# Two graph-attention layers on one core: the softmax's shift and sum folded into 12 segment-wise exponentials, moved to the head of ScalarE's step

## The reference: what is computed

```python
q, k, v = split_heads(x @ Wq + bq), split_heads(x @ Wk + bk), split_heads(x @ Wv + bv)
scores = einsum('bhqd,bhkd->bhqk', q, k) / sqrt(32) + beta * adj
scores = where(adj > 0, scores, -9e15)
x = layernorm(x + einsum('bhqk,bhkd->bhqd', softmax(scores), v))          # layer 0

a = einsum('bnhd,bmhd->bhnm', x @ Wq.T, x @ Wk.T) * 384 ** -0.5 + adj
a = nan_to_num(softmax(where(all(a == 0, axis=-1), -inf, a)))
x = layernorm(x + einsum('bhnm,bmhd->bnhd', a, x @ Wv.T + bv) @ Wo.T + bo)  # layer 1
```

## Time and profile before

| | |
|---|---|
| device time, median of 3 runs | 1110.32 us (1110.06 to 1113.08) |
| device time of the profiled execution | 1110.85 us |
| its span, first to last instruction | 1109.1 us |
| TensorE matmuls busy | 1063.5 us (96%) |
| VectorE busy | 936.5 us (84%) |
| GpSimd busy | 528.7 us (48%) |
| ScalarE busy | 444.9 us (40%) |
| mean granted TensorE clock | 0.985 |

### The profile page before, as it was taken

How to read it: one execution, slowest core, us unless ns; L and a number is a source line. 1 busy time by engine, 2 the same in 40 slices (tenths; PEclk the granted TensorE clock), 3 DMA queues, 4 the chain that set the end, 5 groups by cost and what they waited for, 6 DMA issues and landing times.

```text
span 1109.1 us, 38264 instructions
## 1 busy us (share of the span) xinstructions
PE 1063.5 (96%) x16896; PEld 917.9 (83%) x16896; DVE 936.5 (84%) x1642; ACT 444.9 (40%) x713; POOL 528.7 (48%) x454
## 2 busy tenths in 40 slices
PE   4789999999999999999999999999999999999975
PEld 3678888888888888888888888888888888888864
DVE  2468998998989899898989989898898989978785
ACT  3334443444344343444433444444444434444321
POOL 0135454454545546454454645445364544655443
PEclk8989999999999999999999999999999999999997
DMA  8103111112112011111102111111211210010101
GB/s 265 39 2 97 50 59 43 38 45 64 37 43 59 26 54 46 42 53 49 49 26 64 38 43 59 43 38 45 64 38 43 59 36 15 17 35 2 40 24 37
DMA packets 61749, 53.32 MB, mean 48 GB/s; under 512 B 35984, under 2 KB 55440, under 8 KB 61584
## 3 DMA queue, kind: packets, MB, share of 16 engines
q1 hardware_dynamic: 60752, 49.69, 15.1%
q10 hardware_dynamic: 832, 1.18, 0.3%
HBM read 38.28 MB, written 12.58 MB: 46 GB/s over the span
## 4 chain that ended last, share of the span: by engine, by line
PE 90%; DVE 4%; issue 2%; DMA 2%; ACT 1%; POOL 1%; SPq 0%; POOLq 0%; DVEq 0%; ACTq 0%
PE ps_u L340 53%; PE ps_s L357 9%; PE ps_o L340 8%; PE ps_p L425 7%; PE ps_p L440 7%; PE ps_x L370 3%; PE ps_o L454 2%; DMA xt_in<-in_x_t 1%; DVE probs L620 1%; POOL probs L756 1%; DMA bo_rows<-in_bo 1%; DVE row_sum L668 1%; DVE xt_lo L648 1%; ACT probs L547 0%; DVE row_max L630 0%
## 5 line engine op out<-in xcount | busy, mean ns | idle before, releaser
L756 POOL TENSOR_TENSOR probs<-probs,row_max 128x768 f32<-128x768 f32 x128 | 209.8, 1639 | 323.0 <-DVE row_max L630 323.0
L762 POOL TENSOR_TENSOR probs<-probs,row_inv 128x768 f32<-128x768 f32 x128 | 188.6, 1474 | 128.8 <-DVE row_inv L676 69.5
L516 ACT COPY probs_t<-ps_p 128x768 f32<-128x768 f32 x128 | 102.6, 802 | 201.3 <-PE ps_p L425 201.2
L340 PE MATMUL ps_u<-w_hi_v,xt_lo 128*128 128x384 f32 x384 | 138.4, 360 | 7.0 <-DVE v_sb L661 5.4
L668 DVE TENSOR_REDUCE row_sum<-probs 128x12 f32<-128x768 f32 x128 | 121.6, 950 | 24.4 <-ACT probs L547 23.6
L547 ACT ACTIVATE probs<-probs 128x768 f32<-128x768 f32 x128 | 108.4, 847 | 83.0 <-POOL probs L756 83.0
L340 PE MATMUL ps_u<-xt_hi,w_lo_k 128*128 128x512 f32 x288 | 119.0, 413 | 11.6 <-ACT q_sb L535 6.3
L340 PE MATMUL ps_u<-w_hi_v,xt_hi 128*128 128x384 f32 x384 | 129.9, 338 | 0.0
L340 PE MATMUL ps_u<-w_lo_v,xt_hi 128*128 128x384 f32 x384 | 129.8, 338 | 0.0
L775 POOL TENSOR_TENSOR rstd<-var_eps,minus_half 128x1 f32<-128x1 f32 x128 | 69.9, 546 | 124.9 <-DVE var_eps L709 124.9
L630 DVE TENSOR_REDUCE row_max<-probs 128x12 f32<-128x768 f32 x128 | 121.4, 948 | 2.2
(11 more groups left out here) (78 smaller groups left out, 2033.4 us busy)
## 6 DMA issues: line engine op xcount, KB each, us to landing
x_in<-in_x SPq DMA_DIRECT2D x16, 768.0 KB, 4.5
out<-z SPq DMA_DIRECT2D x64, 192.0 KB, 1.9
xt_in<-in_x_t SPq DMA_DIRECT2D x15, 768.0 KB, 4.7
adj<-in_adj SPq DMA_DIRECT2D x64, 128.0 KB, 2.9
xt_in<-in_x_t SPq DMA_DIRECT2D x3, 256.0 KB, 4.6
q_sb<-in_wq ACTq DMA_DIRECT2D x3, 192.0 KB, 4.8
k_sb<-in_wk ACTq DMA_DIRECT2D x1, 576.0 KB, 7.6
v_sb<-in_wv SPq DMA_DIRECT2D x1, 576.0 KB, 7.2
```

Of the source, the lines that this page charges most:

```text
L340: last = nc.tensor.matmul(dst, a(g), b(g), start=(g == 0 and n == 0), stop=(g == KT - 1 and n == 2))
L516: nc.scalar.copy(probs_t[:].rearrange("p (a i) n -> p a (i n)", a=2), ps_p[:, :, 0:KT * P]).then_inc(probs_t_ready, 1)
L756: nc.gpsimd.tensor_tensor(s, s, over_keys(row_max[p]), ALU.subtract).then_inc(shifted, 1)
L762: nc.gpsimd.tensor_tensor(s, s, over_keys(row_inv[p]), ALU.mult).then_inc(probs_ready, 1)
```

## The change

Row maxima are negated by VectorE as they are taken (`minus_max`). GpSimd's subtraction and VectorE's row sum are gone, with their semaphores. ScalarE's one exponential of 128 x 768 becomes 12 of 128 x 64, each with its own column of `minus_max` as bias and its own column of `row_sum` as accumulator output. They wait for `max_ready` of the current tile, and stand in front of the first unit's eviction and of `probs_out(prev)`.

```diff
-        row_max = [sb(f"row_max{p}", [P, PAIRS * GT]) for p in range(2)]
+        minus_max = [sb(f"minus_max{p}", [P, PAIRS * GT]) for p in range(2)]
...
             def exponentials(tile):
-                act.wait_ge(shifted, at(tile) + 1)
-                e = probs[tile[2] % 2][:].rearrange("p i b k -> p (i b k)")
-                nc.scalar.activation(e, e, ACT.Exp).then_inc(exp_ready, 1)
+
+                p = tile[2] % 2
+                act.wait_ge(max_ready, at(tile) + 1)
+                for i in range(PAIRS):
+                    for b in range(GT):
+                        n = i * GT + b
+                        last = nc.scalar.activation(probs[p][:, i, b, :], probs[p][:, i, b, :], ACT.Exp,
+                                                    bias=minus_max[p][:, n:n + 1],
+                                                    accum_out=row_sum[p][:, n:n + 1])
+                last.then_inc(exp_ready, 1)
...
                 if s.turned:
                     activations_hi(s.turned)
+                if s.cur:
+                    exponentials(s.cur)
                 for unit in s.units[:1]:
                     unit_out(unit)
                 if s.prev:
                     probs_out(s.prev)
-                if s.cur:
-                    exponentials(s.cur)
                 for unit in s.units[1:]:
                     unit_out(unit)
...
-                nc.vector.tensor_reduce(row_max[t % 2][:], rows, AX_X, ALU.max).then_inc(max_ready, 1)
+                nc.vector.tensor_reduce(minus_max[t % 2][:], rows, AX_X, ALU.max, negate=True).then_inc(max_ready, 1)
...
                 dve.wait_ge(exp_ready, at(tile) + 1)
-                nc.vector.reduce_sum(row_sum[p][:], probs[p][:].rearrange("p i b k -> p (i b) k"), AX_X)\
-                    .then_inc(sum_ready, 1)
-                dve.wait_ge(sum_ready, at(tile) + 1)
...
-            def shift(tile):
-                p = tile[2] % 2
-                pool.wait_ge(max_ready, at(tile) + 1)
-                s = probs[p][:].rearrange("p i b k -> p (i b) k")
-                nc.gpsimd.tensor_tensor(s, s, over_keys(row_max[p]), ALU.subtract).then_inc(shifted, 1)
...
             for s in STEPS:
-                if s.cur:
-                    shift(s.cur)
                 if s.turned:
                     add_bo(s.turned)
```

More of the change, by code:

```diff
@@ L222, in two_gnn_layers_kernel @@
         v_ready = sem("v_ready")
-        sum_ready = sem("sum_ready")
         inv_ready = sem("inv_ready")
@@ L231, in two_gnn_layers_kernel @@
         normed = sem("normed")
-        shifted = sem("shifted")
         probs_ready = sem("probs_ready")
```

## The result

The changed kernel takes 1372.59 us (median of 4 runs, 1372.19 to 1375.94) against 1111.7 us before (median of 4 runs, 1110.06 to 1113.78): 1.2352 times as long, 95% interval 1.232 to 1.2384. The forecast was slower, 1550 us with a range of 1205 to 1640. The profiled execution has a span of 1370.6 us, 261.5 us more than before.

The account below looks back on a forecast made before the run. TensorE, gapless in the steady part, was taken as the bound. To 1110.85 us came 391 for waits on ScalarE, accumulator included (1502), and 49 for falls of the clock: 1550 us, range 1205 to 1640.

Parts of the forecast that it names:

- TensorE's gapless work: Steady part: TensorE busy 65.65 of 65.66 us in eight steps, so relieving VectorE and GpSimd is worth nothing there.
- TensorE's due times and the new waits: When TensorE asks for ScalarE's evictions and copies, against their delivery: six waits, 6.35 us in eight steps without the accumulator.
- The segments: ScalarE's 12 small exponentials: about 0.243 us each, 2.92 us to the next instruction, where 0.75 stood.
- The accumulator: A second small ScalarE instruction for each segment's sum, not overlapped: 0.20 us each, 2.4 us a step.
- the group of eight: One turn of each layer, eight steps: 24.46 us of added waits, 16 such groups making 391 us.
- The clock: TensorE falls to half clock behind long waits: two falls in eight steps at 1.52 us each, 49 us in all.
- The sum: Whole kernel: 1110.85 us plus 391 of waits gives 1502, and with 49 for the clock 1550 us.
- faster: Rival: segments start so closely (0.11 us each) that no steady step waits and the ends gain 8 us: 1103, chance 0.03.
- no change: Rival: no steady step waits and the gain at the ends is hidden behind other work: 1110 us, chance 0.03.
- The half price: Rival: the accumulator's instruction overlaps its exponential, costing 0.10 us a segment: 1349 us, chance 0.18.
- The signs: Expected in the trace: segments 0.44 us apart, TensorE's share about 70%, waits in six to eight steps of eight.

Follow-up runs that it names:

- two_wide: Kernel before, with two 128x384 exponentials a tile, each graph's maximum as bias, no GpSimd shift, VectorE sums, still behind the copy of `probs_t`: 1099.84 us.
- keep_busy: Changed kernel plus 10 to 14 idle transposes on TensorE in front of what waits for ScalarE, at five of eight steps: 1355.83 us.
- two_wide_head: two_wide with its two exponentials at the head of ScalarE's step, as in the change: 1148.16 us, ratio 1.034 to the kernel before.
- late_bias: Changed kernel with the bias of layer 0's next turn made at the end of VectorE's step t = 1 of layer 1's turn: 1377.83 us.

## Why the prediction was right in direction and too high

- **TensorE's gapless work** was read too simply. The prediction held relief of VectorE and GpSimd to be worth nothing in the steady part; two_wide's eight steps take 65.02 us instead of 65.66, so small waits stood there. It changes the forecast by nothing, as the waits of the changed kernel are far longer.
- **TensorE's due times and the new waits** held. With the measured accumulator (0.09, or 1.08 us a step) in the prediction's list, the waits are 0.82, 1.90, 2.61, 2.19, 2.65 and 2.07 where the trace has 0.85, 1.82, 2.56, 2.41, 2.70 and 1.99. The reckoned 0.25 at layer 0's t = 0 and 1.41 at layer 1's t = 2 don't show in this stretch, since a fall of the clock has just slowed TensorE in both; in keep_busy, without falls, they are there, 0.18 and 1.36.
- **The segments**: 2.92 reckoned (from 0.243 a segment, where the rows as printed give 0.246), 2.88 measured without the accumulator.
- **The accumulator** is the term that was mis-sized. The trace shows a second instruction, 187 ns long. The Trainium skill states such a second instruction for VectorE ("VectorE: DVE Perf Modes", "Two Vector instructions with no wait between them"); here it is ScalarE's. But the read overlaps at both ends and adds 0.09 us, the case that the prediction priced at 0.10 and gave 0.18. The reason for 0.20, that a write of a complete sum has nothing to overlap with, was wrong. With 1.08 instead of 2.4 the group of eight is 0.25 + 0.82 + 6.35 + 6 x 1.08 = 13.90, or 222 us in place of 391.
- **The clock**: two falls in eight steps were counted, and two there are, 24 in the 12 steady pairs of turns: in the stretch shown behind waits of 2.70 and 1.99 us, in the next pair at waits of 2.43 and 2.70, so not at the longest alone. The price was 1.52 us, and keep_busy gives 0.7: much of the slowed work lies where TensorE would have waited anyway, and of `heads` and scores only a part runs slow.
- **The sum** with both measured: 1110.85 + 222 + 17 = 1350, 22 us under the result. Of these, 10 are in the 12 steady pairs: keep_busy's eight steps take 80.42 us against 65.66 + 13.90 = 79.56, and the seam alone has 0.22 more wait than reckoned. The other 12 lie at the two ends, which are 67 us longer than before where four groups were reckoned with 56; no run separates what is in them.
- **The rivals**: faster and no change are ruled out. The half price came nearest (1349): its accumulator is the measured one within 0.01 us, and that the falls it leaves out cost little was luck.
- **The signs**: segments 0.33 us apart lie between the 0.44 and 0.24 named. TensorE's share fell to 82%, not 70%, with 1129 us busy. TensorE's longest waits are where they were named, at layer 0's t = 3 and layer 1's t = 1. ScalarE's wait for the maxima is 261.9 us in 127 waits, 2.1 each, as said.

## What to carry to other kernels

Before moving an instruction ahead in a queue, ask what it waits for and what stands behind it: here an exponential that waits for the newest scores was put ahead of evictions that needed only old ones, and the move alone cost 129 us with no work added. With a shorter chain from the maxima the same move cost nothing in seven steps of eight, and 2 to 4 us in the eighth, where VectorE was late with the maxima. Relief of engines that TensorE hardly waits for is worth little: without the shift, two_wide gained 9 us, and here 377 us less of VectorE and GpSimd work bought nothing. To fold a maximum into an exponential's bias, choose the widest span that may share one maximum: in the same old place, 2 instructions of 384 columns made the kernel 1% faster, 12 of 64 made it 7% slower, and 12 with accumulators 12%.

## What the runs showed of the hardware that was not expected

- The accumulator output of a ScalarE exponential is an instruction of its own, 187 ns long and 0.09 us in net, though the program has one instruction.
- A VectorE subtraction of two SBUF tensors, 128 x 384, is three times as fast without GpSimd's shift beside it: mean 1681 ns before, in the changed kernel 551. Before, the 53 that started while a shift ran took 1.83 us, the 7 others about 0.55:

```profile
L648 DVE TENSOR_TENSOR xt_lo<-xt_in,xt_hi 128x384 fp32r<-128x384 f32 x60 | 100.8, 1681 | 10.7 <-ACT xt_hi L510 10.7
```

```profile
L653 DVE TENSOR_TENSOR xt_lo<-xt_in,xt_hi 128x384 fp32r<-128x384 f32 x60 | 33.0, 551 | 11.8 <-ACT xt_hi L508 11.8
```

  Likewise the bias's first instruction takes 1.51 us in the rows of two_wide_head and 0.42 in those of late_bias; GpSimd's scaling (L761 and L760) ran beside the first, from 627.52 to 628.99, and had ended a microsecond before the second, at 681.63. The bias is on the path of the changed kernel: at the seam it stands ahead of the maxima, and its first instruction takes 1.50 us there, as in the kernel before from which the wait was reckoned:

```profile
657.96 1.50 DVE L593 TENSOR_SCALAR bias<-adj 128x512 f32<-128x512 f32 x1
```

- The clock fell behind waits of 2.70 and 1.99 us in the changed kernel and not behind one of 3.01 us before, so the length of one wait did not decide it.
